# A decoder layer's prologue in another order: adapter products, softmax halves, query spread and waits

## The reference

```python
x = x + attn(layernorm(x), wq, wk, wv, wo)       # causal, 32 query heads of 16, 8 key/value heads
x = x + xattn(layernorm(x), ctx, Wq_d, W_qk, Wkv_d, Wv_u)
...
    C_kv = ctx @ Wkv_d                            # latents, 32 wide
    CqWqk = ((Q @ Wq_d) @ W_qk)                   # 16 heads of 32
    attn = softmax(CqWqk @ C_kv.T / sqrt(32))
    out = attn @ (C_kv @ Wv_u)
...
x = x + ffn(layernorm(x))
    A_eff, B_eff = gate @ lora_A, gate @ lora_B   # the adapter products, one per group of two batch elements
    out = h @ kernel + bias + (h @ A_eff) @ B_eff + (h @ lora_A_shared) @ lora_B_shared
```

## Time and profile before

| what | us |
|---|---|
| median of 3 runs (lowest, highest) | 678.75 (678.68, 680.32) |
| the profiled execution | 681.57 |
| its span, first to last instruction | 679.6 |
| first maxima of `body(0)` in it | 64.66 |
| mean granted TensorE clock (share of full) | 0.947 |

### The profile page before, as it was taken

One profiled execution on the slowest core, in us unless ns is written; L12 is line 12 of the kernel. 1 busy time (PEld: TensorE's weight loads), 2 busy tenths in 40 slices (PEclk: granted clock), 3 DMA queues, 4 the chain that ended last, 5 costly groups with the idle time before them and its releaser, 6 DMA issues.

```text
span 679.6 us, 12918 instructions
## 1 busy us (share of the span) xinstructions
PE 591.6 (87%) x3856; PEld 306.8 (45%) x3856; DVE 442.2 (65%) x717; ACT 303.8 (45%) x641; POOL 424.9 (63%) x394
## 2 busy tenths in 40 slices
PE   4863988699999999998999999999999899986965
PEld 4331644353544554464456354455446444433322
DVE  2711796378776887489658867588758966745451
ACT  1330144335644374346534564337444744563450
POOL 5002027558965886598776896488659877789300
PEclk9895889799999999999989999999999999997896
DMA  8567630353116510481018311661048101100000
GB/s 310 211 210 245 236 119 18 78 210 166 43 29 228 211 44 1 115 323 57 17 42 271 154 43 31 225 215 43 1 130 333 32 15 47 43 9 1 22 1 14
DMA packets 31410, 77.22 MB, mean 114 GB/s; under 512 B 11378, under 2 KB 25042, under 8 KB 28915
## 3 DMA queue, kind: packets, MB, share of 16 engines
q1 hardware_dynamic: 31186, 75.36, 33.1%
q10 hardware_dynamic: 160, 1.05, 0.4%
HBM read 58.66 MB, written 2.88 MB: 91 GB/s over the span
## 4 chain that ended last, share of the span: by engine, by line
PE 62%; DVE 12%; issue 7%; POOL 6%; ACT 5%; SPq 3%; DMA 3%; POOLq 0%; ACTq 0%; DVEq 0%
PE st_ps L649 11%; PE mx_ps L677 10%; PE pv_ps L664 9%; POOL acc L1096 5%; PE mi_ps L459 4%; PE mi_ps L466 4%; PE mi_ps L453 4%; PE mi_ps L512 4%; SPq L371 3%; PE mi_ps L631 2%; DVE mx_p L1020 2%; DVE sm L982 2%; PE mi_ps L537 2%; DMA b_eff<-acc 2%; PE mi_ps L635 2%
## 5 line engine op out<-in xcount | busy, mean ns | idle before, releaser
L1096 POOL TENSOR_TENSOR acc<-acc,p_ring 125x448 f32<-125x448 f32 x300 | 359.8, 1199 | 49.2 <-ACT p_ring L833 23.5
L1020 DVE TENSOR_REDUCE mx_p<-mx_ps 128x1 f32<-128x500 f32 x336 | 210.7, 669 | 101.7 <-PE mx_ps L677 100.6
L833 ACT ACTIVATE p_ring<-st_ps 125x448 f32<-125x448 f32 x384 | 189.7, 544 | 171.4 <-PE st_ps L649 164.4
L649 PE MATMUL st_ps<-q_st,c_st 98*125 98x448 f32 x384 | 155.3, 432 | 13.4 <-ACT p_ring L833 7.7
L677 PE MATMUL mx_ps<-c_st,q_st 96*128 96x500 f32 x336 | 139.4, 446 | 14.9 <-DMA q_st<-q_hl 11.2
L649 PEld LDWEIGHTS st_ps<-q_st,c_st 98*125 98x125 f32 x384 | 68.7, 191 | 117.1 <-ACT p_ring L833 88.2
L1104 POOL TENSOR_TENSOR rstd<-mv,eps_col 128x1 f32<-128x1 f32 x24 | 4.6, 192 | 153.2 <-DVE mv L894 153.2
L664 PE MATMUL pv_ps<-p_ring,c_nat 125*32 125x448 f32 x768 | 94.4, 564 | 1.0 <-ACT p_ring L833 0.9
L677 PEld LDWEIGHTS mx_ps<-c_st,q_st 96*128 96x128 f32 x336 | 63.2, 196 | 41.4 <-issue 20.6
L1096 POOL TENSOR_TENSOR acc<-p_ring 125x448 f32<-125x448 f32 x30 | 36.6, 1221 | 27.3 <-ACT p_ring L833 27.3
L466 PE MATMUL mi_ps<-ctx_sb,wkv_sb 128*32 128x375 f32 x512 | 48.1, 496 | 0.7 <-DVE p L943 0.7
(11 more groups left out here) (111 smaller groups left out, 671.0 us busy)
## 6 DMA issues: line engine op xcount, KB each, us to landing
ctx_sb<-in_ctx_t SPq DMA_DIRECT2D x16, 3000.0 KB, 11.1
c_st<-ct_hl SPq DMA_DIRECT2D x192, 46.9 KB, 2.0
q_st<-q_hl SPq DMA_DIRECT2D x96, 56.0 KB, 2.0
x_sb<-in_x SPq DMA_DIRECT2D x16, 112.0 KB
out_y<-x3n SPq DMA_DIRECT2D x16, 112.0 KB
wq_sb<-in_wq SPq DMA_DIRECT2D x2, 512.0 KB, 4.4
ctx_sb<-in_lora_a SPq DMA_DIRECT2D x1, 1024.0 KB, 6.8
ctx_sb<-in_lora_b SPq DMA_DIRECT2D x1, 1024.0 KB, 8.7
```

What stands on the lines that cost most here:

```text
L649: mm(st_ps[unit % STB][0:KC, 0:HALF], c_st[:, b % 4, t * KT + k * KC:t * KT + (k + 1) * KC], q_st[:, b // 2 % 2, b % 2, half * HALF:(half ...
L833: act.activation(p_ring[:, unit % PR, :], st_ps[unit % STB][0:KC, 0:HALF], ACT.Exp, scale=float(L) ** -0.5).then_inc(exp_done, 1)
L1020: ve.tensor_reduce(mx_p[:, p:p + 1], mx_ps[unit % MXB][:, 0:KP], AX.X, ALU.max).then_inc(red_done, 1)
L1096: po.tensor_tensor(dst, first, p_ring[:, unit % PR, :].rearrange("p (h s) -> p h s", s=S), ALU.add).then_inc(acc_done, 1)
```

## The change

- SP: `x` comes in DRAM with the gaps between the slots filled, so that a pair is one DMA of 128 partitions and DVE's fill of `x_sb` is dropped, and SP's wait for it. `wk` moves ahead of `wq`; context 0 moves ahead of the adapters' inputs; the load of x for pair 1 moves from `body(0)` into the prologue. `spread_q(0)` no longer waits for `eff_out`; SP issues six of its 12 DMAs behind `load_ctx(1)`, and ACT issues the other six behind its copy to `q_hl`. The `eff_out` wait of SP moves to the end of `body(0)`.
- PE: 16 products of the identity with itself ahead of T1. The adapter products stand in four places: two behind P1, one behind O1, four behind W1, one behind T2. The waits for `w_ffn` and the bias move to the end of `body(0)`, and PE waits for `CST_MADE` instead of `ALL_MADE`.
- ACT: a one-element exponential at the start. A's copy stands between the two exponentials of the softmax. The adapter copies follow the products. The two stores come behind the six query DMAs, and the `eff_out` wait moves to the first exponential of `body(0)`.
- DVE: S0, S1, SM0, S2, S3, SM1 in place of S0 to S3, SM0, SM1. The factor `gkron` moves to POOL.
- POOL: the first power comes behind the masks; the fill of `acc` and its `eff_out` wait move into `body(0)`.

```diff
+        def spread_first_q(dma, part, dst, t):
+
+            dma(q_st[dst:dst + L, 0, :, t * 4 * S:(t + 1) * 4 * S].bitcast(F32),
+                q_hl[t * L:(t + 1) * L, part, :, :].bitcast(F32)).then_inc(q_in[0], 16)
...
-                for h in range(2):
-                    dma(x_sb[h * SLOT:h * SLOT + S, n % 2, :], x[pair_index(n), h]).then_inc(x_in[n % 2], 16)
+                dma(x_sb[:, n % 2, :], x[pair_index(n)].rearrange("b s d -> (b s) d")).then_inc(x_in[n % 2], 16)
...
-            sp.wait_ge(dve_c, due(dve_c, 1))
             load_x(0)
...
+            load_ctx(0)
+            dma(g8[:, :], gate_t).then_inc(raw_in, 16)
             for k in range(2):
                 dma(lora_raw[k], (lora_a, lora_b)[k].rearrange("n (e f) r -> (n e) (f r)", e=8)).then_inc(raw_in, 16)
-            dma(g8[:, :], gate_t).then_inc(raw_in, 16)
-            load_ctx(0)
             dma(wo_sb[:, :, :], wo.rearrange("(r p) n -> p r n", p=128)).then_inc(w_out, 16)
+            load_x(1)
...
             sp.wait_ge(lora_ps, due(lora_ps, 8))
             load_ctx(1)
+
+            sp.wait_ge(qh_hi, due(qh_hi, 1))
+            for t in range(4):
+                spread_first_q(dma, 0, 0, t)
+            for t in range(2):
+                spread_first_q(dma, 0, L, t)
+
             dma(kern_sb[:, :, :], kern.rearrange("(c p) n -> p c n", p=128)).then_inc(w_ffn, 16)
...
-            sp.wait_ge(eff_out, due(eff_out, 32))
-            spread_q(0)
...
             pe.wait_ge(pool_c, due(pool_c, IDENT_MADE))
+            for _ in range(16):
+                mm(mx_ps[0][:, 0:128], ident[:, :], ident[:, :], start=True, stop=True)
             step("T1", 0)
...
-            for name in ("Ah", "A", "V", "CT"):
+            for name in ("Ah", "A", "V", "CT", "P0", "P1"):
                 step(name, 0)
-            lora_factors(0, 6)
-            for name in ("P0", "P1", "P2", "P3", "O1"):
+            lora_factors(0, 2)
+            for name in ("P2", "P3", "O1"):
                 step(name, 0)
-            lora_factors(6, 8)
+            lora_factors(2, 3)
             pe.wait_ge(w_out, due(w_out, 16))
             step("Wh", 0)
             step("W1", 0)
+            lora_factors(3, 7)
             step("T2", 0)
+            lora_factors(7, 8)
...
-            act.wait_ge(dve_c, due(dve_c, 2))
+            act.wait_ge(dve_c, due(dve_c, 1))
+            act.activation(table[:, :], minus_half[:, :], ACT.Exp)
...
-            for name in ("T1", "Q1", "SE0", "SE1", "A", "V", "CT"):
+            for name in ("T1", "Q1", "SE0", "A", "SE1"):
                 step(name, 0)
...
+            act.wait_ge(qh_hi, due(qh_hi, 1))
+            for t in range(2, 4):
+                spread_first_q(act.dma_start, 0, L, t)
+            act.wait_ge(qh_lo, due(qh_lo, 1))
+            for t in range(4):
+                spread_first_q(act.dma_start, 1, 2 * L, t)
             act.wait_ge(lora_sb, due(lora_sb, 8))
             for k, dst in enumerate((a_eff, b_eff)):
                 act.dma_start(dst.rearrange("i (e f) r -> (i e) (f r)", e=8), lora_eff[k][:, 0:2048])\
                     .then_inc(eff_out, 16)
-            for name in ("T2", "CQ", "H"):
-                step(name, 0)
-            act.wait_ge(eff_out, due(eff_out, 32))
...
-            for name in ("S0", "S1", "S2", "S3"):
-                step(name, 0)
...
-            for name in ("SM0", "SM1", "SN0", "SN1", "AS"):
+            for name in ("S0", "S1", "SM0", "S2", "S3", "SM1", "SN0", "SN1", "AS"):
                 step(name, 0)
```

More of the change, by code:

```diff
@@ L58 @@
 FIRST_LOOPED, LAST_LOOPED = 1, 6
-IDENT_MADE, MASKS_MADE, PADS_MADE, ALL_MADE = 2, 6, 10, 12
+IDENT_MADE, MASKS_MADE, PADS_MADE, CST_MADE, ALL_MADE = 2, 6, 10, 11, 12
 PIECES_IN = [3, 2, 4, 3, 0, 0, 0, 3, 4, 1, 3, 0]
@@ L194, in decoder_layer @@
         minus_half = sb("minus_half", [128, 1])
+        table = sb("table", [128, 1])
         eps_col = sb("eps_col", [128, 1])
@@ L217, in decoder_layer @@
         ab_in = sem("ab_in", 32)
-        for s in x_in + ctx_in:
+        for s in x_in:
+            rates[s.name] = 16
+        for s in ctx_in:
             rates[s.name] = 32
@@ L238, in decoder_layer @@
         dve_c = sem("dve_c", 0)
+        gk_done = sem("gk_done", 0)
         lora_ps = sem("lora_ps", 0)
@@ L385, in store_y @@
                     dma(out[pair_index(n), h], x3n[h * SLOT:h * SLOT + S, :]).then_inc(y_out, 16)
-            sp.wait_ge(dve_c, due(dve_c, 1))
             load_x(0)
+            dma(wk_sb[:, :, :], wk.rearrange("(c p) n -> p c n", p=128)).then_inc(w_attn, 16)
             for c in range(2):
@@ L418, in _ @@
             dma(b_sb[2 * RANK:2 * RANK + 1, :], bias).then_inc(y_out, 16)
-            sp.wait_ge(eff_out, due(eff_out, 32))
-            spread_q(0)
             def body(i):
                 if 2 * i + 2 < B:
-                    load_x(i + 1)
+                    if i:
+                        load_x(i + 1)
                     load_ctx(2 * i + 2)
@@ L439, in body @@
                             store_y(n)
+                if i == 0:
+                    sp.wait_ge(eff_out, due(eff_out, 32))
             run_bodies(sp, at, body)
@@ L680, in lora_factors @@
             def lora_factors(since, until):
-                pe.wait_ge(raw_in, due(raw_in, 16 * 3))
-                pe.wait_ge(dve_c, due(dve_c, 4))
+                pe.wait_ge(gk_done, due(gk_done, 1))
                 for q in range(since, until):
@@ L713, in _ @@
                 step(name, 0)
[L714 to L715 removed]
             pe.wait_ge(lora_sb, due(lora_sb, 8))
[L717 removed]
+            pe.wait_ge(pool_c, due(pool_c, CST_MADE))
             def body(i):
@@ L734, in body @@
                         step(name, n, i, g)
+                if i == 0:
+                    pe.wait_ge(w_ffn, due(w_ffn, 16 * 3))
+                    pe.wait_ge(y_out, due(y_out, 16))
             run_bodies(pe, at, body)
@@ L824, in exponentials @@
                 half = g // KG
+                if b == 0 and g == 0:
+                    act.wait_ge(eff_out, due(eff_out, 32))
                 for t in range(4):
@@ L849, in lora_out @@
                         .then_inc(lora_sb, 1)
-            for name in ("T1", "Q1", "SE0", "SE1", "A", "V", "CT"):
+            for name in ("T1", "Q1", "SE0", "A", "SE1"):
                 step(name, 0)
-            lora_out(0, 6)
-            for name in ("P0", "P1", "P2", "P3", "O1"):
+            act.wait_ge(dve_c, due(dve_c, 2))
+            for name in ("V", "CT", "P0", "P1"):
                 step(name, 0)
-            lora_out(6, 8)
+            lora_out(0, 2)
+            for name in ("P2", "P3", "O1"):
+                step(name, 0)
+            lora_out(2, 7)
+            step("T2", 0)
+            lora_out(7, 8)
+            for name in ("CQ", "H"):
+                step(name, 0)
+            act.wait_ge(qh_hi, due(qh_hi, 1))
[4 more added lines that the diff above has]
+                spread_first_q(act.dma_start, 1, 2 * L, t)
             act.wait_ge(lora_sb, due(lora_sb, 8))
@@ L907, in step @@
                 if name == "L0":
-                    ve.wait_ge(x_in[slot], due(x_in[slot], 32 * (n // 2 + 1)))
+                    ve.wait_ge(x_in[slot], due(x_in[slot], 16 * (n // 2 + 1)))
                     statistics(0, n, x_sb[:, slot, :])
@@ L1132, in _ @@
             assert made[0] == MASKS_MADE
+            po.wait_ge(dve_c, due(dve_c, 1))
+            power(0, 0)
             make(po.memset(ones[:, :], 1.0))
@@ L1139, in _ @@
             make(po.memset(c_st[96:98, :, :].bitcast(F32), 1.0))
+            assert made[0] == CST_MADE
+            po.wait_ge(raw_in, due(raw_in, 16 * 3))
+            po.wait_ge(dve_c, due(dve_c, 3))
+            po.tensor_tensor(gkron[:, :, :], g8[:, :].unsqueeze(2).to_broadcast([128, PAIRS, 8]),
+                             e8[:, :].unsqueeze(1).to_broadcast([128, PAIRS, 8]), ALU.mult).then_inc(gk_done, 1)
             power(1, 0)
-            po.wait_ge(eff_out, due(eff_out, 32))
-            make(po.memset(acc[:, :, :, :], 1.0))
-            assert made[0] == ALL_MADE
             def body(i):
                 power(0, i + 1)
+                if i == 0:
+                    po.wait_ge(eff_out, due(eff_out, 32))
+                    make(po.memset(acc[:, :, :, :], 1.0))
+                    assert made[0] == ALL_MADE
                 if i < PAIRS:
@@ L1169 @@
     arrays = {
-        "x": a["x"].reshape(PAIRS, 2, S, D),
+        "x": np.pad(a["x"].reshape(PAIRS, 2, S, D), ((0, 0), (0, 0), (0, SLOT - S), (0, 0))),
         "ctx_t": a["ctx_4096"].transpose(0, 2, 1),
```

9 lines of the change are left out of this document (1 added, 8 removed).

## The result

The changed kernel takes 692.65 us (median of 4, 688.98 to 693.74) against 679.54 for the kernel before on the same chip: 1.0179 times as long, 95% interval 1.0138 to 1.0221 (the quotient of the two medians is 1.0193). I had forecast 668.6. The profiled execution took 692.17 with a span of 690.0.

A forecast was written before the change was run, and what follows sets the result against it. Bound: the prologue's waits up to the first maxima, with SP waiting for the adapters' store ahead of the queries. First maxima at 54.6 for 64.66, 10.1 earlier, off 678.75 gives 668.6; range 664 to 673, bounds 665.2 to 677.2.

The forecast's parts named there:

- bodies as long as before: Sign for the nine bodies behind the prologue: their lengths stay, so what the first maxima gain, the end gains.
- The prologue's own steps: Prologue up to `q_hl`: S0 at 15.0 (-3.0), P2 at 31.4 (-5.5), T2 at 42.5, `q_hl` at 46.7 (-7.4).
- the latents: Latents on PE in the prologue: start at 21.5, take 2.73, plus 1.3 for slowness, bounds 0 and 2.7.
- the weights: Attention weights for K in the prologue: arrive 1.6 earlier, by 9.0, and do not bind; K at 9.4.
- The best start: Bound for the prologue up to S0: identity products of 3.9 and fast K and Q, 1.2 more gained.
- the widest gain: Upper bound at the first maxima: best start 1.2, no slow latents 1.3, copies not held 1.0; 13.6, time 665.2.
- The query spread: From `q_hl` to first maxima: split issues 3.9, landing 2.0, but held by context 1 (10.2) until 54.6 for 64.66.
- not held: Rival: SP's six query copies land in 2.0 us beside context 1; gain 12.5 to 13.6, 665.7; chance 0.12.
- SP stands: Rival: SP's first query issue stands behind context 1 and goes out at 52.3; gain 6.5, 672.3; chance 0.10.
- The moved waits: Waits, stores and POOL's fill of `acc` moved into or toward the first body: cover of 24 us, cost nothing.
- The rival "slower": ACT's first exponential in the first body waits for stores landing after 87; 689 if at 57 us; chance 0.03.

The follow-up runs named there:

- the run with clean spreads: Changed kernel with 15 more instructions on SP and 194 more on PE, all waits already met: 694.15 us, ratio 1.0216 to the kernel before.
- 48 products: Changed kernel with 48 small products more on PE ahead of the bodies, read by nothing: 689.46 us, ratio 1.0151 to the kernel before.
- 113 on SP in before: Kernel before with 113 more instructions on SP (waits already met) ahead of its wait for the eighth adapter product: 681.99 us, ratio 1.0040.
- all three places: Changed kernel without the identity products, with 15 more instructions on SP and 2 more on DVE: 679.08 us, ratio 1.0001 to the kernel before.
- fill later: As all three places, with POOL's fill of acc also waiting until DVE has made xn of pair 1: 675.70 us, ratio 0.9925 to before.
- before with the identity products: Kernel before with only the 16 identity products added ahead of its T1: 684.60 us, ratio 1.0060 to the kernel before.
- two on DVE: Changed kernel with two more instructions on DVE (waits already met) ahead of its wait for W1: 685.29 us, ratio 1.0070 to the kernel before.
- without the identity products: Changed kernel without the 16 identity products ahead of T1: 688.78 us, ratio 1.0107 to the kernel before.
- 126 on DVE in before: Kernel before with 126 more instructions on DVE (waits already met), no other edit: 687.23 us, ratio 1.0142 to the kernel before.
- x in two loads: Changed kernel with x loaded by two DMAs again in place of one: 697.11 us, ratio 1.0227 to the kernel before.
- 15 on SP: Changed kernel with 15 more instructions on SP (waits already met) ahead of its wait for the eighth adapter product: 690.73 us, ratio 1.0162.
- context 1 behind the copies: Changed kernel with SP's load of context 1 behind the six query copies instead of ahead: 697.62 us, ratio 1.0290 to the kernel before.

## Why the prediction was wrong

**The step that failed** is in its first paragraph: "The nine bodies follow from there and are not edited but for the load of x, so what the first maxima gain, the end gains". It put the cost in the loop at nothing, and its sign "bodies as long as before" is the one that failed. The source of the bodies was as before; their place in each engine's program was not. Shown by the runs: a different place of DVE's loop code gives back 7 us in the changed kernel and costs 8 to 10 in the one before; the identity products, which move PE's by 62, cost the kernel before 4.1 (0.6%), although its first maxima came earlier with them; DVE, SP and PE set back (and the identity products gone) leave no loss in the loop. The mechanism of the largest part by the times, from the rows: at one place DVE is 0.12 late, POOL's sum goes first, and the subtraction, ACT and PE pay 0.9 to 1.0 each time, often with PE's clock at half behind it (in the run with clean spreads PE stood 1.48 at 327.4, and the granted clock was 0.50 from 328.4 to 335.3). DVE's subtraction and POOL's sums took 1.09 and 6.47 in one order, 1.99 and 5.54 in the other.

The subtraction is not the whole loss. Stretches 3 and 5 of all fourteen profiled kernels, sorted by the two places (a slow issue is one of 0.99 us or more in the spread that opens the stretch; 48 products stand in two lines, with the stretch in brackets):

| in the stretch | of kernels | length, us |
|---|---|---|
| neither | before, 113 on SP in before, all three places, fill later | 73.3 to 73.9 |
| slow issue alone | before with the identity products, two on DVE | 73.8 to 79.5 |
| slow subtraction alone | without the identity products, 48 products (5), 15 on SP with 194 on PE, 126 on DVE in before | 74.5 to 77.0 |
| both | changed, x in two loads, 48 products (3), 15 on SP, context 1 behind the copies | 76.4 to 81.1 |

Within a row the time at the clock's lower level goes with the length: with a slow subtraction alone, 74.5 and 74.7 where the clock never fell, 75.3 with 3.4 us of it, 76.6 to 77.0 with 6.8.

Why a row comes late at one place of an engine's program is not shown. Measured are these: SP's late rows stand 128 apart. DVE's row maximum starts 0.22 to 0.46 behind the small subtraction in bodies 1, 3 and 5 of the changed kernel, 0.10 in all three with two instructions more, and 0.19 to 0.45 in the kernel before with 126 more. Slow issues coincide with queue 8's packets, which moved into the spread when PE's program alone was made longer; within 50 rows at the loop's end the changed kernel has three of them.

**The prologue's own steps** were right to 0.1 to 0.8 us up to `q_hl`, in part because errors met: the latents took 4.42, 1.7 over the 2.73 where I had added 1.3, but started at 20.68 and not 21.5. K did wait 0.78 for the weights, which I had not had bind. The best start was summed wrongly: with the weights there at 9.0, K comes 0.4 earlier than in the sum, not 1.2, and the widest gain is 12.8, not 13.6. **The query spread** was mis-sized, by 4.4: context 1 went out 0.6 earlier than I had it but took 12.7 and not 10.2, and the last copy landed 2.8 behind it where I had 0.3. That the copies are held was right (the rival "not held" was wrong), but ACT's, which I had land at 52.6, were held too. "SP stands" was wrong: its first query issue took 0.68. **The moved waits** were not free: the fill of `acc`, put beside `xn`, cost body 0 some 4 us in the kernel with all places set back. ACT's wait for the stores cost nothing: they landed at 60.5. **The rival "slower"** named the outcome and the wrong mechanism. The chance of slower, 0.03, left out that a prologue edit can move the loop.

Open: what the places of ACT (8) and POOL (1) do; how much of SP's place counts by itself; and why stretch 1 takes 75 us even when all is in place. In stretch 1 PE's clock stands at 0.50 for 8 to 11 us where the subtraction takes 1.09, before included, and in stretches 3 and 5 of the undisturbed kernels for 0 to 2; what makes it fall there was not followed.

## What to carry to other kernels

An edit ahead of a hardware loop can change the time of the loop without touching it (by 15.7 us in bodies 1, 3 and 5 here): compare the lengths of the rounds first, and if all rounds but not all bodies are longer, count how far each engine's loop code has moved and pad it back before judging the edit. Look at places where two engines meet within a tenth of a microsecond (here DVE's subtraction, 1.09 or 1.99 us, and POOL's sums, 6.47 or 5.54): who is first there can be decided by code that is nowhere near. And a small transfer that is issued beside a large load can take far longer, on either queue: 8.1 to 8.4 us here beside context 1, and 2.0 to 2.1 ahead of it.

## What the runs showed of the hardware

- Two instructions more on DVE ahead of a loop made the changed kernel, of 692 us, 7 us faster.
- An issue of a DMA on SP took 1.0 to 2.0 us instead of 0.60 where it coincided with a 16 KB packet of instructions on queue 8. Not every such issue did: without the identity products one beside such a packet took 0.69.
- A DVE subtraction with two SBUF inputs took 1.09 us when it started 0.04 ahead of a POOL sum, and 1.99 when the sum started 0.10 ahead of it.
- 56 KB copies took 8.1 to 8.4 us beside a 3,000 KB load, on the load's own queue and on another, and 2.0 and 2.1 when the load came behind them.
- A fill of `acc` on POOL made DVE's 0.54 us `xn` take 3.23.
- 388 waits that were already met, 194 instructions on PE, filled 20.7 us ahead of the first maxima, by estimate some 0.1 us an instruction; the first maxima came 6.8 us later than in the changed kernel.
